# Attention with a routed feed-forward on one core: projection moved behind the value blocks, and some masking moved from GpSimd to VectorE

## The reference, cut to what is computed

```python
# x: (16, 256, 128) float32; 16 heads of 8; 7 routed experts and one shared, inner size 352, top 2
xn = layernorm(x)
def attention(xn):
    q, k, v = heads(einsum('bte,fe->btf', xn, in_proj_weight))
    a = einsum('bhtd,bhkd->bhtk', q / sqrt(8), k) + causal_mask      # -inf where key > query
    return einsum('bte,fe->btf', merge(einsum('bhtk,bhkd->bhtd', softmax(a), v)), out_proj_weight)
def ffn(xn):
    out = expert(xn, sg, su, sd)
    w = top-2 of softmax(xn @ wr.T + rb), normalised to sum 1
    for e in range(7):
        out += w[..., e:e+1] * expert(xn, rg[e], ru[e], rd[e])       # silu(h @ g.T) * (h @ u.T) @ d.T
    return out
return x + attention(xn) + ffn(xn)
```

## Time and profile before

| | |
|---|---|
| median of 3 runs | 512.21 us (511.63 to 515.35) |
| the profiled execution | 512.13 us |
| its span, first to last instruction | 510.1 us |
| mean granted TensorE clock | 0.935 |
| busy in the span: TensorE, VectorE, ScalarE, GpSimd | 90%, 69%, 60%, 58% |

### The profile page before, as it was taken

One profiled execution on the slowest core, in us unless ns is written; L12 is line 12 of the kernel. 1 busy time (PEld: TensorE's weight loads), 2 busy tenths in 40 slices (PEclk: granted clock), 3 DMA queues, 4 the chain that ended last, 5 costly groups with the idle time before them and its releaser, 6 DMA issues.

```text
span 510.1 us, 12198 instructions
## 1 busy us (share of the span) xinstructions
PE 458.3 (90%) x3919; PEld 328.0 (64%) x3923; DVE 350.2 (69%) x722; ACT 306.4 (60%) x661; POOL 296.1 (58%) x424
## 2 busy tenths in 40 slices
PE   8888998989878887878898999989899999979996
PEld 4766555646555554555565667868668788858874
DVE  6796998868766565665555048757667687656897
ACT  2756776757665565665555667646547676546653
POOL 1445997968767567667677540255364497856300
PEclk9999999979998699898756699999999999989999
DMA  9786999897753454355237024767767668730762
GB/s 249 234 256 216 317 317 308 289 377 252 249 158 110 124 147 153 96 159 152 89 106 273 22 86 141 228 207 226 242 210 247 223 195 279 246 119 28 227 196 72
DMA packets 60412, 99.80 MB, mean 196 GB/s; under 512 B 11045, under 2 KB 29226, under 8 KB 59328
## 3 DMA queue, kind: packets, MB, share of 16 engines
q1 hardware_dynamic: 55872, 90.57, 56.0%
q0 software_dynamic: 4480, 8.47, 4.9%
HBM read 60.85 MB, written 38.94 MB: 196 GB/s over the span
## 4 chain that ended last, share of the span: by engine, by line
PE 65%; ACT 8%; issue 5%; SPq 5%; another core or an unknown queue 5%; DVE 4%; DMA 2%; ACTq 0%; DVEq 0%; POOL 0%
PE ps L894 11%; PE ps L892 11%; PE ps L893 10%; PE ps L1042 6%; PE ps L975 6%; PE ps L983 5%; ACT sb_work L767 3%; PE ps L1046 3%; PE ps L1025 2%; PE ps L1210 2%; SPq L494 2%; PE ps L971 2%; PE ps L1027 2%; DMA sb_ring<-qk 2%
## 5 line engine op out<-in xcount | busy, mean ns | idle before, releaser
L1416 DVE TENSOR_REDUCE sb_blockmax<-ps 128x6 f32<-128x768 f32 x128 | 121.3, 955 | 67.2 <-PE ps L983 61.9
L767 ACT ACTIVATE sb_work<-ps 128x768 f32<-128x768 f32 x128 | 104.0, 813 | 79.2 <-PE ps L971 60.8
L663 POOL DMA_INDIRECT ys<-sb_v_all,sb_xn_all x76 | 79.3, 1043 | 76.0 <-DVE sb_v_all L1543 57.1
L635 POOL TENSOR_SCALAR_AFFINE_SELECT sb_work<-sb_work 128x512 f32<-128x512 f32 x128 | 82.2, 643 | 56.1 <-ACT sb_work L767 54.7
L893 PE MATMUL ps<-sb_ring,sb_wb 128*128 128x512 f32 (+5 forms) x231 | 83.2, 360 | 0.0
L975 PE MATMUL ps<-sb_ring 32*128 32x256 f32 x256 | 53.0, 406 | 29.4 <-ACT sb_work L767 23.2
L1521 DVE TENSOR_TENSOR sb_v_all<-ps,sb_v_all 128x512 f32<-128x512 f32 (+3 forms) x93 | 57.2, 615 | 25.7 <-ACT sb_v_all L839 10.4
L613 POOL DMA_INDIRECT xs<-sb_xn_all,sb_posu x64 | 62.2, 972 | 13.7 <-issue 13.7
L975 PEld LDWEIGHTS ps<-sb_ring 32*128 32x128 f32 x256 | 26.5, 196 | 60.3 <-issue 52.1
L983 PE MATMUL ps<-sb_mask_b,sb_ident_b 128*128 128x256 bf16 x256 | 55.1, 301 | 0.0
L839 ACT ACTIVATE sb_v_all<-ps 128x512 f32<-128x512 f32 (+3 forms) x93 | 49.5, 532 | 9.0 <-PE ps L894 5.4
(11 more groups left out here) (165 smaller groups left out, 1063.0 us busy)
## 6 DMA issues: line engine op xcount, KB each, us to landing
sb_wb<-wd SPq DMA_DIRECT2D x50, 384.0 KB
sb_ring<-qk SPq DMA_DIRECT2D x64, 256.0 KB
wd<-sb_wb SPq DMA_DIRECT2D x8, 1088.0 KB, 5.2
sb_wb<-wd SPq DMA_DIRECT2D x25, 320.0 KB
xs<-sb_o_all SPq DMA_DIRECT2D x19, 260.0 KB, 3.6
qk<-sb_ring SPq DMA_DIRECT2D x32, 128.0 KB
sb_work<-ys SPq DMA_DIRECT2D x16, 256.0 KB, 3.2
sb_xn_all<-xs SPq DMA_DIRECT2D x15, 260.0 KB
```

Of the source, the lines that this page charges most:

```text
L635: pool.affine_select(out=o, in_=o, compare_op=ALU.is_ge, fill=0.0, base=0, pattern=[[0, 4], [1, 128]], channel_multiplier=-1)\
L663: pool.indirect_dma_start(out=ys_d, out_offset=bass.IndirectOffsetOnAxis(ap=row, axis=0), in_=yst[i % NYS][:, EMB * j:EMB * j + EMB], in_o ...
L767: act.activation(part.rearrange("p (k h q) -> p h k q", h=2, q=128), ps[:, 4:6, 0:HEAD].rearrange("p h (k q) -> p h k q", q=128), ACT.Exp, ...
L1416: dve.tensor_reduce(blockmax[:, p % 2, q, a:b + 1, 0:3], ps[:, a:b + 1, 0:HEAD].rearrange("p h (k c) -> p h k c", c=128), AX.X, ALU.max).t ...
```

## The change

Three things change. In TensorE's steps from 0 on, both value blocks of quad n - 1 now always stand together ahead of the second half of the scores, and `project(n)` moves to the very end of the step. The two copies that empty the projection (`projection_high` on ScalarE, `projection_low` on VectorE) accordingly move from step n to step n + 1. And from step 24 on, the first of the two selections of each even step (20 steps, 24 to 62) leaves GpSimd: VectorE does it between its two maxima as a minimum of the exponentials with a constant (3.4e38 kept side, 0 masked side) that adds 128 columns to the constants' load.

```diff
-C_ALL = C_DEC + ROUTED
+C_KEEP = C_DEC + ROUTED
+C_ALL = C_KEEP + 128
...
+    c[:, C_KEEP:C_KEEP + 128] = np.where(p[:, None] <= p[None, :], 3.4e38, 0.0)
...
+        N_KEEP = range(N_SEND + 1, NQ, 2)
+
+        def selected(n):
+
+            return 2 * n + 2 - len([k for k in N_KEEP if k <= n])
...
                 if isq(n):
-                    for k in range(2):
+                    for k in range(n in N_KEEP, 2):
                         pair = PAIRS[1 - k]
                         pool.wait_ge(s["ex"], 2 * n + k + 1)
...
                     for k, pair in enumerate(PAIRS[::-1]):
-                        if k and projected(n) is not None:
-                            projection_high(n)
+                        if k and n and projected(n - 1) is not None:
+                            projection_high(n - 1)
...
-                    pe.wait_ge(s["sel"], 2 * n + 2)
+                    pe.wait_ge(s["sel"], selected(n))
+                    if n in N_KEEP:
+                        pe.wait_ge(s["kept"], N_KEEP.index(n) + 1)
...
-                if projected(n) is not None:
+                if n < 0 and projected(n) is not None:
                     project(n)
                 if isq(n - 1):
                     value_sums(n - 1, 0)
-                    if projected(n) is None:
-                        value_sums(n - 1, 1)
+                    value_sums(n - 1, 1)
                 if isq(n) or isq(n + AHEAD):
                     scores(n, 1)
-                if isq(n - 1) and projected(n) is not None:
-                    value_sums(n - 1, 1)
                 if 0 < n < NQ + 2 and n % 2:
                     across(n)
                 if n >= 0 and isq(n + 2):
                     maxima(n + 2)
+                if n >= 0 and projected(n) is not None:
+                    project(n)
...
-                if n >= 0 and projected(n) is not None:
-                    projection_low(n)
+                if n > 0 and projected(n - 1) is not None:
+                    projection_low(n - 1)
                 if n in N_ROUTE:
                     next(route)
+                if n in N_KEEP:
+                    dve.wait_ge(s["ex"], 2 * n + 1)
+                    o = P[n % 2][:, HEAD * PAIRS[1][0]:HEAD * PAIRS[1][0] + 512].rearrange("p (k q) -> p k q", q=128)
+                    dve.tensor_tensor(o, o, const[:, C_KEEP:C_KEEP + 128].unsqueeze(1).to_broadcast([128, 4, 128]),
+                                      ALU.min).then_inc(s["kept"], 1)
```

More of the change, by code:

```diff
@@ L365, in build @@
         s_std = sem("s_std")
-        names = ("pq pk hq hk lq lk S max0 max1 mhi mx Mt q4b ST ex sel PV OT T xc rc nm busy "
+        names = ("pq pk hq hk lq lk S max0 max1 mhi mx Mt q4b ST ex sel kept PV OT T xc rc nm busy "
                  "xn xa nb xp xT xh xl V va lg tT oT wcp wsp rs var0 var rt rx selb id0 id1 cnts cnt pos tabs "
```

## The result

The changed kernel took 514.41 us in the median of 15 executions (507.89 to 518.54), the kernel before 512.21 us in 15 (505.58 to 519.64): a ratio of 1.0083, interval 1.0046 to 1.012. The forecast was 511.7 us, 0.1% faster. The measured time lies in the range (505.5 to 517), but the change costs about 4.2 us by the ratio where I had forecast a gain of 0.4. The means over all 15 executions are 514.2 and 512.0 us, 2.2 us apart; the same kernel measured again in run 1 lies 4.3 us above the kernel before by the means. So there is a loss, and its size is known to some 2 us. The profiled execution of the changed kernel took 512.97 us, with a span of 511.2 us.

A forecast was written before the change was run, and what follows sets the result against it. It took SyncE's DMA queue to bound 72 to 107 us and GpSimd's queue the later step pairs. Terms -0.5, -0.5, +0.5, +0.1 and zeros gave -0.4 us on 512.13: 511.7 us, range 505.5 to 517.

The forecast's parts named there:

- the term for SyncE's queue: Step 13's store waits for the late low copy, delaying the reload queued behind it: 0 to +1.5 us, +0.5 taken.
- the held pairs: Step pairs from 24 on, where the odd exponential is timed from the even one and the hold takes any gain: 0.
- the half-clock part: Three or four projecting steps at half clock, where TensorE is the bound and its saved 0.14 us counts: -0.5 us.
- The two value blocks and the projection: TensorE's reordered steps: second exponential up to 0.20 us earlier in free even steps, a free pair gaining about 0.24 us.
- the sum's two -0.5 terms: Gains of TensorE's new order: -0.5 us in two pairs between 107 and 129 us, -0.5 us at half clock.
- held even steps: The 13 projecting even steps from 24 to 48: second exponential 0 to 0.20 us earlier each, 0 to -2.6, 0 taken.
- The copies one step later: Both projection copies fit ScalarE's and VectorE's gaps in odd steps: no cost, at most 0.41 us per odd step.
- The minimum and the constants: Minimum hidden between VectorE's two maxima in 20 even steps: 0; 64 KB more constants loaded ahead of the inputs: +0.1 us.
- The hold: Odd steps: ScalarE idles 1.79 us before its exponential, beside GpSimd's second consecutive send and a selection; forecast to stay.
- the first rival: Hold is GpSimd's selection behind a send; removing it frees even steps from 24 on: 505.3 us, chance 0.17.
- The second rival: SyncE's late stores delay reloads at steps 5 and 13 and lengthen seven odd-step holds: 5.8 us, 517.5 us, chance 0.14.
- The third rival, the clock: Half-clock stretches begin after TensorE's idle times and could grow or shrink: 508 to 515.5 us, chance 0.14.

The follow-up runs named there:

- run 4: Changed kernel, but from step 1 on SyncE issues the heads' store behind the same step's reload; 0.9959 of the kernel before.
- run 16: Repeat of the changed kernel with the store issued behind the same step's reload; 0.9930 of the kernel before.
- run 13: New order and late copies in all steps, without the minimum, store issued behind the same step's reload; 0.9958 of the kernel before.
- Run 5: Kernel before, only with the store issued behind the same step's reload from step 1 on; 1.0039 of the kernel before.
- run 9: Kernel before with TensorE's order kept, only the two copies that empty the projection one step later; 1.0001 of the kernel before.
- run 15: Repeat of the kernel before with only the two projection copies one step later; 0.9990 of the kernel before.
- run 6: Kernel before with the new order and late copies only from step 24 on, all selections on GpSimd; 1.0059 of the kernel before.
- Run 8: Kernel before, but from step 24 on each step's first indirect send stands between its two selections; 0.9540, 482.7 against 507.0 us.
- run 2: Changed kernel with its new order and late copies, but all selections back on GpSimd; 1.0092 of the kernel before.
- run 10: Kernel before with both value blocks together behind the projection, which keeps its place, copies in the same step; 1.0026 of the kernel before.
- run 12: Changed kernel with the store behind the reload and the sends apart from step 24 on; 0.9548 of the kernel before, mean 491.4 us.
- run 11: Kernel before in its old order, with sends apart and the minimum on VectorE; 482.43 us in the median, 0.9446 of the kernel before.

## Why the prediction was wrong, step by step

**The step that failed is the term for SyncE's queue.** I priced it at step 13 alone, 0 to +1.5 us, and took +0.5, because "the reload lands 7.93 us behind its issue with DMA engines 92% busy, so most of a later issue is spent in a backlog that is there anyway". I saw what was queued behind the store and read the backlog as cover. Runs 4, 16 and 13 put the value of getting the reload out of that queue, in the new order, at 1.2% (1.0079 to 0.9959), 1.5% (to 0.9930) and 1.3% (1.0092 to 0.9958). By the means over all executions it is 1.0 to 1.2%: 5 to 6 us in place of 0.5. What failed in it is the number of places and the cover, not the delay at step 13. The store leaves 2.97 us later there (89.46 to 92.43), but the exponential of step 12 is already 1.82 us late (86.00 to 87.82), so step 13 itself adds 1.15 us, inside the 0 to 1.5 that I gave. The same wait stands in earlier steps, for which the sum had nothing: the stores of steps 1 and 5 leave 2.05 and 2.37 us later (49.35 and 63.18, before 47.30 and 60.81), though steps 0 and 4 are not late. And the backlog was no cover: in this trace the reload issued 1.12 us later landed 2.20 us later. How the 5 to 6 us divide between these two, the runs don't show.

The runs shift the question more than they close it. Run 5 shows that the store's place costs nothing in the old order; so the store matters only together with something in the new one. The late copies, which make the store wait, don't bring the 0.9% by themselves (runs 9 and 15). What else of the new order it takes is open, and whether the late half's 2.6 us (run 6) come by the stores too was not tried: my sum had 0 for the held pairs and -0.5 for the half-clock part there.

**The two value blocks and the projection.** In a free even step the exponentials come closer, by less than computed. Those of step 12, in the changed kernel and in the kernel before:

```profile
87.82 0.81 ACT L775 ACTIVATE sb_work<-ps 128x768 f32<-128x768 f32 x1 [0.87 <-PE ps L979]
89.31 0.81 ACT L775 ACTIVATE sb_work<-ps 128x768 f32<-128x768 f32 x1 [0.68 <-PE ps L979]
...
86.00 0.81 ACT L767 ACTIVATE sb_work<-ps 128x768 f32<-128x768 f32 x1 [1.71 <-PE ps L971]
...
87.63 0.81 ACT L767 ACTIVATE sb_work<-ps 128x768 f32<-128x768 f32 x1 [0.54 <-PE ps L971]
```

They are 1.49 us apart, and 1.63 before: 0.14 us less, where the forecast was 0.20. With the store out of the way the order stands at 0.9958 [0.9915,1.0001] (run 13; by all executions 0.2% faster). That agrees with the sum's two -0.5 terms, and with no gain as well. In held even steps the forecast of "0 to -2.6 us" had no loss in it: step 26 became 0.27 us longer.

**The copies one step later**: cost 0 forecast, 0.9990 and 1.0001 measured, by the means 1.6 and 2.3 us slower. Neither 0 nor 2 us is refuted. The price that they cause by the stores stood in the SyncE term.

**The minimum and the constants**: 0 and +0.1 forecast, 0.9999 measured, for both at once; 684 ns for one where I took 638, in the slot that I named.

**The hold.** That "the idle time before ScalarE's exponential stays at 1.8 to 2.0 us" in odd steps came true in step 27 (1.80). What it is, I had half: the first rival took it for GpSimd's selection behind a send. Run 8 has a selection behind every send, and step 27 starts 0.04 us behind its scores; and in the changed kernel step 26 has no selection behind its send and is held 0.49 us. So that rival's mechanism was false, and its time (505.3) as well. What the release goes with is a send that started shortly before it; two in a row make it long.

**The second rival** named SyncE's stores, the reloads of steps 5 and 13, and 517.5 us, at a chance of 0.14. It was nearest to what happened, though the loss was less than its 5.8 us. Its 0.4 us more hold in late odd steps isn't there: the odd step 27 became 0.08 us shorter. But the late half alone does cost (1.0059).

**The third rival, the clock.** Over 118 executions of the kernel before, mean clock and time go together: 0.01 less clock goes with 1.8 us more (a line through them, correlation -0.77), and without a single execution at 0.833 with 2.8 us more. In runs 1 and 2 the clock is 0.019 and 0.016 lower than that of the kernel before in the same series, which would go with 3.5 and 2.8 of their 4.3 and 4.2 us by the first line, and with all of it by the second; in run 10 it is 0.010 lower, which would go with all of its 1.8 us. In runs 4 and 16 it is 0.009 and 0.002 lower, and they are faster by 1.0 and 1.8 us. So the kernels with the new order have the lower granted clock. Whether the clock is a cause of the time or follows from the same waits, no run here separates, and this rival stays open. I had named "a mean clock off by more than 0.01" as a sign of being wrong, and that sign came.

## What to carry to other kernels

An instruction that waits in a queue can cost what is behind it, at every occurrence and not only where the chain shows it now: look up every place where the queue's wait gets later, and try the waiting instruction behind the urgent one. Don't take a backlog of transfers for a cover of a later issue without a run that shows it. Where a step shows an idle time that the named releaser doesn't explain, take the engine beside it apart: here two instructions exchanged on an engine that the view of the waits didn't name were worth more than five times what the change cost. And where executions scatter as much as the effect, one trace of each kernel doesn't locate a loss.

## What the runs showed of the hardware

*An indirect DMA issued by GpSimd can hold back the release of TensorE's finished work, and two in a row do it longest.* A matmul that ended at 143.30 us let ScalarE start at 144.94, 1.64 us behind it and 1.58 us behind the second send's start (143.36). In run 12 it was 161.23 to 162.89, 1.54 us behind the second send's start. With a selection of 0.62 us between the sends, ScalarE started 0.04 us behind its matmul (140.91 to 140.95, run 8). A single send can hold as well: in step 26 of the changed kernel the scores ended at 139.92, 1.22 us behind the send's start, and were released at 140.41, 1.71 behind it; in run 8 the release at 214.72 came 1.58 us behind a single send's start. And two in a row need not hold for long: in step 32 of run 11 the release came 0.39 us behind the matmul (158.95 to 159.34), with sends at 158.00 and 159.29. So the separating selection may help only because the next send starts later; the runs don't separate the two readings, and in some places a matmul that ended early in a send was released at once (run 8, 226.79 us, 0.16 behind the send's start). Why this is so, the traces don't tell.

*The granted clock was lower where the holds were.* The stretch from 160 to 240 us ran at 0.88 in the kernel before and 0.87 in the changed one, a mix of 2.4 and 1.2 GHz; in both the long holds leave TensorE idle (1.47 us ahead of the scores at 144.21, just behind the one of the earlier trace rows). It ran at 1.00 in runs 8 and 11, and at 0.89 in run 12, which has three of its four long holds there. The mean over the execution rose from 0.95 to 0.98 in runs 8 and 11.
